# A two-stage layer on one core: the attention half's engine orders from a table of steps with due times

## The reference

```
q_top, q_idx = top_k(x @ w_qr[g], 512);  queries    = x[q_idx]     # 512 of 1024 tokens
kv_top,kv_idx= top_k(x @ w_kvr[g],256);  key_values = x[kv_idx]    # 256 tokens
q = queries @ w_q[g].T;  k, v = split(key_values @ w_kv[g].T);  v *= sigmoid(kv_top)
k, v get one learned null row;  attn = softmax(q k^T / 8)          # 8 heads of 64
o = (attn v) @ w_out[g].T * sigmoid(q_top)
result[q_idx] += o / number of groups that chose the token; tokens chosen by none get null_token
```

## Time and profile before

| | us |
|---|---|
| median of 3 runs | 3996.88 (3987.88 to 4007.33) |
| profiled execution | 3995.63 |
| its span | 3994.3 |

### The profile page before, as it was taken

The page is one execution under the profiler, slowest core; times in us unless marked ns, Lnnn a source line. Parts: engine busy times, 40 slices in busy tenths (PEclk is TensorE's granted clock), DMA queues, the critical chain, the costliest instruction groups (busy, mean ns, idle before and its releaser), DMA issues. The chain is left out here.

```text
span 3994.3 us, 72425 instructions
## 1 busy us (share of the span) xinstructions
PE 3649.7 (91%) x28354; PEld 2154.7 (54%) x28354; DVE 2955.1 (74%) x5374; ACT 2549.6 (64%) x4781; POOL 1770.5 (44%) x1483
## 2 busy tenths in 40 slices
PE   4899999999999999998568899988999989999998
PEld 2455555555555555555335455555555555656554
DVE  4788888888888888879756666666766666767663
ACT  4677676777777776765335655657665666656565
POOL 0232323333232333323336777656555565555555
PEclk8899999999999999999779999999999999999998
DMA  4223332324233332332343433334333343333332
GB/s 122 69 72 82 76 74 51 85 72 86 72 86 69 78 78 59 77 70 47 62 74 64 96 66 74 73 69 101 67 74 72 80 90 77 70 65 76 70 64 36
DMA packets 297670, 294.28 MB, mean 74 GB/s; under 512 B 38664, under 2 KB 223624, under 8 KB 295281
## 3 DMA queue, kind: packets, MB, share of 16 engines
q1 hardware_dynamic: 241008, 186.70, 18.8%
q0 software_dynamic: 56320, 102.94, 14.7%
HBM read 176.19 MB, written 101.71 MB: 70 GB/s over the span
## 5 line engine op out<-in xcount | busy, mean ns | idle before, releaser
L1542 DVE SCALAR_TENSOR_TENSOR cv<-raw,taps,cv 128x512 f32<-128x512 f32 x480 | 427.2, 900 | 70.1 <-ACT cv L1950 66.7
L1792 DVE TENSOR_REDUCE smx<-pair 128x2 f32<-128x514 f32 x512 | 346.3, 683 | 87.5 <-PE pair L1330 70.8
L2231 POOL TENSOR_TENSOR ph<-pf,ph 128x512 f16<-128x512 f32 x256 | 307.5, 1202 | 211.2 <-ACT ph L2090 210.2
L1149 PE MATMUL pair<-xhT,whi 128*128 128x512 f16 x1280 | 383.1, 381 | 0.2
L1397 PE MATMUL pair<-whi,oT 128*128 128x512 f16 x1024 | 333.2, 388 | 1.1 <-issue 0.7
L2236 POOL TENSOR_TENSOR ohl<-of,ohl 128x256 f16<-128x256 f32 x256 | 184.6, 721 | 332.3 <-ACT ohl L2095 332.1
L1195 PE MATMUL pair<-whi,xhT 128*128 128x512 f16 x1024 | 325.7, 379 | 0.2 <-DVE gmask L1581 0.2
L1232 PE MATMUL pair<-ohi,yT 128*128 128x512 f16 x1024 | 318.8, 383 | 1.1 <-ACT yT L2007 1.1
L1289 PE MATMUL pair<-xq,whi 128*128 128x512 f16 x1024 | 313.5, 388 | 3.0 <-ACT kb L2022 3.0
L1731 DVE TENSOR_SCALAR_CACHE_REDUCE rjunk<-rbc,cst 128x640 f16<-128x640 f16 (+1 forms) x192 | 185.5, 966 | 175.8 <-DMA rbc<-rank 169.7
L1980 ACT ACTIVATE de<-de,cum 128x128 f32<-128x128 f32 x1024 | 309.7, 389 | 1.0
(11 more groups left out here) (248 smaller groups left out, 10441.1 us busy)
## 6 DMA issues: line engine op xcount, KB each, us to landing
de<-cum SPq DMA_DIRECT2D x64, 1024.0 KB, 9.3
rows<-rowt SPq DMA_DIRECT2D x16, 1040.0 KB, 5.4
xin<-x SPq DMA_DIRECT2D x16, 1024.0 KB, 7.4
y<-xin SPq DMA_DIRECT2D x16, 1024.0 KB, 4.5
y<-ob POOLq DMA_DIRECT2D x64, 256.0 KB, 4.3
rbc<-rank SPq DMA_DIRECT2D x64, 256.0 KB, 3.8
qb<-qa SPq DMA_DIRECT2D x32, 512.0 KB
ka<-ka SPq DMA_DIRECT2D x32, 256.0 KB
```

The costliest lines, as they stand in the source:

```text
L1149: ins = pe.matmul(bk[:], w[:, k, ws], xt[:, ha, k, :], start=n == 0, stop=n == 3 * KD - 1)
L1542: ve.scalar_tensor_tensor(c_[:], r_[:, t:t + BLK], taps[:, ct, t:t + 1], c_[:], ALU.mult, ALU.add).then_inc(done, 1)
L1792: ve.tensor_reduce(smx[:, qt, 2 * h2:2 * h2 + 2], sc[:, :, 0:NK + 1], AX.X, ALU.max)
L2231: po.tensor_tensor(p_[:, 1, 1], f[:, 1], p_[:, 0, 1], ALU.subtract).then_inc(S.plp, 1)
```

## The change

The attention half is recorded as PE steps alone (`Feed` into a `Record`), and the new `arrange_items` gives `Order` all other steps of all 32 items in one table, with durations, inputs, readers of banks and landing times. Every step of one name runs in the order of the table. `Order` gets `keep`: a reader of a bank is also due `KEEP` = 4.0 us after the end of the PE step that it reads; for the Mamba half it is 1e9. `route`, `split_weights`, `null_rows` and the `last_q`, `last_k`, `last_max` steps go. The VectorE copy of null key columns has its own name, `keys_null`; VectorE's half of the low probabilities is `low_v`; ScalarE's cast is a step `high_p` of its own. The share at which the maxima begin goes from -1.25 to -0.8 (end 1.1 as before), and in the prologue the rows of item 1 come behind the maxima of item 0.

```diff
--- before.py
+++ after.py
 SCALE = DH ** -0.5
 LAG = 2
 SLOP = 0.7
+KEEP = 4.0
...
-    def __init__(self, plan, done, taken=(), between=()):
+    def __init__(self, plan, done, taken=(), between=(), keep=1e9):
+        self.keep = keep
...
-        follow = {}
-        for step, (_, _, after, _, _) in self.nodes.items():
+        follow, held = {}, {}
+        for step, (_, us, after, seats, _) in self.nodes.items():
             for a in after:
                 follow.setdefault(a, []).append(step)
+            for _, readers in seats:
+                for r in readers:
+                    held[r] = starts[step] + us + self.keep
 
         def last_start(step):
             if step not in starts:
                 end = min((last_start(f) for f in follow.get(step, ())), default=t + 100.0)
+                end = min(end, held.get(step, end))
                 starts[step] = end - self.HOP - self.nodes[step][1] - self.nodes[step][4]
...
+def arrange_items(plan, line):
+    done = [("weight_low", 0, NSP - 1), ("nulls", 0), ("slot", 0)]
+    for j in range(RT):
+        done += [(name, 0, j) for name in ("rank", "gather", "row", "row_out")]
+    order = Order(plan, done, keep=KEEP)
+    latest = {}
+    def add(engine, us, step, after=(), seats=(), extra=0.0):
+        after = [a for a in after if a[1] >= 0]
+        if engine != "PE" and step[0] in latest:
+            after.append(latest[step[0]])
+        latest[step[0]] = step
+        order.add(engine, us, step, after, seats, extra)
+    def each(name, n, count):
+        return [(name, n, k) for k in range(count)]
+    def back_by(name, n, h, k):
+        return (name, *divmod(H * n + h - k, H))
+    seats = {"q": "q_low", "k": "k_low", "v": "v_low", "row": "row_out", "max": "max_out", "shift_turn": "shift_out",
+             "null_turn": "null_out", "score": "soft", "value": "norm_o", "oturn": "oturn_out", "out": "res"}
+    takes = {"q": 2.6, "k": 2.62, "v": 2.6, "row": 0.45, "max": 0.23, "shift_turn": 0.24, "null_turn": 0.24,
+             "score": 0.88, "value": 0.95, "oturn": 0.45, "out": 2.6}
+    for step in line:
+        name, n, k = (*step, 0)[:3]
+        if name == "row":
+            after = [("gather", n, k)]
+        elif name in "qkv":
+            after = each("row_out", n, RT) + [("weight_low", n // NB, NSP - 1)]
+        elif name == "max":
+            after = each("q_low", n, KD) + [("keys", n)] + ([("keys_null", n)] if n % NB < 2 else [])
+        elif name == "shift_turn":
+            after = [("shift", n)]
+        elif name == "null_turn":
+            after = [("null_split", n)]
+        elif name == "score":
+            after = each("k_low", n, KT) + [("q_again", n), ("shift_in", n)]
+        elif name == "value":
+            after = [("low_p", n, k), ("low_v", n, k), ("null_out", n), ("nulls", n // NB)] + each("v_low", n, KT)
+        elif name == "oturn":
+            after = [("o_low", n, H - 1)]
+        else:
+            after = [("oturn_out", n, k)]
+        add("PE", takes[name], step, after, [("pair" if name in ("max", "score") else "single", [(seats[name], *step[1:])])])
+    for g in range(1, G):
+        for k in range(NSP):
+            add("SP", 0.5, ("weight_in", g, k), [("weight_low", g, k - 2) if k > 1 else ("weight_low", g - 1, NSP - 1)], extra=4.0)
+            add("ACT", 1.25, ("weight_high", g, k), [("weight_in", g, k), ("out", NB * (g - 1) - 1, QT - 1)])
+            add("POOL", 1.3, ("weight_low", g, k), [("weight_high", g, k)])
+        add("SP", 1.0, ("null_in", g), [("nulls", g - 2)], extra=3.0)
+        add("DVE", 3.3, ("nulls", g), [("null_in", g), ("value", NB * (g - 1) - 1, H - 1)])
+    for b in range(NB):
+        for c in range(TPS):
+            add("POOL", 1.6, ("null_add", b, c), [("score", b, c)], extra=3.0)
+    for n in range(ITEMS):
+        if n:
+            for j in range(RT):
+                if j in (0, QT):
+                    add("SP", 0.5, ("rank_load", n, j // QT), [("rank", n, j - 1) if j else ("slot", n - 1)], extra=3.5)
+                add("DVE", 1.05, ("rank", n, j), [("rank_load", n, j // QT), ("rank", n, j - 1) if j else ("slot", n - 1)])
+            add("DVE", 0.2, ("slot", n), [("rank", n, RT - 1)] + each("store", n - NSLOT, QT) + each("qscore", n - 2, QT) + each("gather", n - 4, RT))
+            for j in range(RT):
+                add("POOL", 1.05, ("gather", n, j), [("slot", n), ("row", n - 1, j), ("row_out", n - 1, j)], extra=4.0)
+                add("ACT", 0.6, ("row_out", n, j), [("row", n, j), ("q", n - 1, KD - 1) if j < QT else ("v_low", n - 1, KT - 1)])
+        two = ("score", n - 2, H - 1)
+        for e in range(KD):
+            add("ACT", 1.2, ("q_out", n, e), [("q", n, e), two])
+            add("DVE", 1.4, ("q_low", n, e), [("q_out", n, e)])
+        add("SP", 0.5, ("q_again", n), each("q_out", n, KD) + [two], extra=4.5)
+        for e in range(KT):
+            add("ACT", 1.2, ("k_out", n, e), [("k", n, e), two])
+            add("DVE", 1.4, ("k_low", n, e), [("k_out", n, e)])
+            add("ACT", 0.7, ("v_out", n, e), [("v", n, e), ("row_out", n, RT - 1), ("value", n - 2, H - 1)])
+            add("DVE", 0.75, ("v_low", n, e), [("v_out", n, e)])
+        add("SP", 0.5, ("keys", n), each("k_out", n, KT) + [two], extra=4.0)
+        if n % NB < 2:
+            add("DVE", 1.2, ("keys_null", n), [("nulls", n // NB), ("max", n - 2, QT * H // 2 - 1)])
+        for k in range(QT * H // 2):
+            add("DVE", 0.84, ("max_out", n, k), [("max", n, k)] + [("null_p", n - 1)])
+        add("DVE", 0.5, ("shift", n), each("max_out", n, QT * H // 2) + [("shift_turn", n - 1), ("null_split", n - 1)])
+        add("DVE", 0.42, ("shift_out", n), [("shift_turn", n), ("shift_in", n - 1)])
+        add("SP", 0.5, ("shift_in", n), [("shift_out", n), two], extra=3.0)
+        add("ACT", 0.25, ("null_p", n), [("shift", n)])
+        add("DVE", 0.65, ("null_split", n), [("null_p", n), ("null_turn", n - 1)])
+        add("DVE", 0.42, ("null_out", n), [("null_turn", n), ("value", n - 2, H - 1)])
+        for h in range(H):
+            add("ACT", 1.05, ("soft", n, h), [("score", n, h), back_by("low_p", n, h, 2), back_by("low_v", n, h, 2)])
+            add("ACT", 1.05, ("high_p", n, h), [("soft", n, h), back_by("value", n, h, LAG + 1)])
+            add("POOL", 1.2, ("low_p", n, h), [("high_p", n, h)])
+            add("DVE", 1.0, ("low_v", n, h), [("high_p", n, h)])
+            add("DVE", 0.66, ("norm_o", n, h), [("value", n, h), back_by("o_low", n, h, 2)])
+            add("ACT", 0.42, ("o_high", n, h), [("norm_o", n, h)] + each("oturn", n - 1, QT))
+            add("POOL", 0.7, ("o_low", n, h), [("o_high", n, h)])
+        for qt in range(QT):
+            add("POOL", 1.05, ("qscore", n, qt), [("slot", n)] + each("res", n - 2, QT), extra=4.0)
+            add("ACT", 0.6, ("oturn_out", n, qt), [("oturn", n, qt), ("out", n - 1, qt)])
+            before = ("store", n, qt - 2) if qt > 1 else ("store", n - 1, QT - 2 + qt)
+            add("ACT", 0.7, ("res", n, qt), [("out", n, qt), before] + each("qscore", n, QT))
+            add("POOL", 1.6, ("store", n, qt), [("res", n, qt)] + each("store", n - NB, QT) + (each("null_add", n, TPS) if n < NB else []), extra=4.0)
+    order.run()
...
-    def split_weights(g):
-        for k in range(NSP + 2):
-            if k > 1:
-                yield ("weight_high", g, k - 2)
-                yield Pause(0.3)
-                yield ("weight_low", g, k - 2)
-                yield Pause(0.5)
...
-        yield ("last_q", n)
...
-            if 0 < h <= QT:
-                yield ("qscore", n, h - 1)
...
     plan.append(("attention",))
-    plan.apart = False
-    for gen in (route(1), prepare(0), turn_rows(1), maxima(0)):
-        feed(gen, 1).to(1)
-        plan.settle()
+    plan.settle()
+    record = Record()
+    for gen in (prepare(0), maxima(0), turn_rows(1)):
+        Feed(gen, 1, record).to(1)
     for n in range(ITEMS):
         others = []
         if n:
-            others.append(Part(feed(turn_out(n - 1), QT * 0.43), -2.9, 6.0))
+            others.append(Part(Feed(turn_out(n - 1), QT * 0.43, record), -2.9, 6.0))
         if n + 1 < ITEMS:
-            others.append(Part(feed(prepare(n + 1), 20.8), 0, 1.8))
-            others.append(Part(feed(maxima(n + 1), 10.2), -1.25, 1.1))
+            others.append(Part(Feed(prepare(n + 1), 20.8, record), 0, 1.8))
+            others.append(Part(Feed(maxima(n + 1), 10.2, record), -0.8, 1.1))
         if n:
-            others.append(Part(feed(finish(n - 1), 10.4), -1.0, 1.0))
+            others.append(Part(Feed(finish(n - 1), 10.4, record), -1.0, 1.0))
         if n + 2 < ITEMS:
-            others.append(Part(feed(route(n + 2), 2 * RT + 3), 0, 1.8))
-            others.append(Part(feed(turn_rows(n + 2), RT * 0.43), -1.9, 1.25))
-        if n < NB:
-            others.append(feed(null_rows(n), TPS))
-        if n % NB == 2 and n // NB + 1 < G:
```

(23 more changed lines are left out.)

## The result

The changed kernel takes 3891.9 us against 3993.2 us: ratio 0.974, 95% interval 0.971 to 0.977. The forecast was 3919, within 3868 to 3972. The profiled execution took 3891.2 us, 104.4 less than that of before.

A forecast was written before the change was run, and what follows sets the result against it. TensorE is busy 91%; the attention half loses 97.3 us against quiet items. Savings of 39 + 15 + 12 + 12 = 78 us off the profiled 3995.6 give 3917.6, plus 1.3 for the median: 3919 us, range 3868 to 3972.

The forecast's parts named there:

- Weights: Items splitting the next group's weights: of 56.9 us lost, 39 us go as pieces spread over ScalarE's idle time.
- Items with null rows: Five items where GpSimd adds null rows lose 17.7 us; two thirds, 12 us, were to go.
- Quiet items: Rank compares waiting for loads in VectorE's queue: 0.4 us less per item, 12 us over 31.
- Null keys and the rest: Maxima's waits for VectorE's null-key copy, 14 us, plus 1 us for the first two items: 15 us saved.
- Maxima earlier: Maxima's share from -1.25 to -0.8: taken as 0, with a key-copy margin of 0.2 us.
- the early maxima's rival: Key copy starts 1 us later, so the first maximum waits 1 us in each of 31 items: 3950 us, 12%.
- Banks: Banks given on when their reader ends in the table, not after a fixed hold: 0, bounds -5 and +31 us.
- Start and end: Item 1's rows move behind item 0's maxima: 0, within 3 us either way; the drain stays.
- no interval above 62 us: Sign for the weights gain: no interval between TensorE's shift transposes, which mark the items, exceeds 62 us.
- this sign of being wrong: ScalarE's weight scaling still waiting over 2 us each for its DMA would show the forecast wrong.
- GpSimd's busy sum: Sign in the changed kernel's profile: GpSimd's and ScalarE's busy sums stay as before.
- The rival from the Trainium skill: VectorE's low-probability halves blocked behind GpSimd's on shared ports, 0.4 us per head: 4020 us, slower, 7%.

The follow-up runs named there:

- e1: Changed kernel with the maxima's share back at -1.25 instead of -0.8: 3937.4 us, ratio 0.995 to the kernel before.
- e4: Kernel before, with only the split of the next group's weights spread over four items instead of one: 3960.1 us, ratio 1.000.
- e9: Changed kernel with the next group's weight loads held back, so the split falls into item 2 as before: 3875.4 us, ratio 0.979.
- e3: Kernel before, with only the null-key copy made its own step ahead of the query projections: 3949.1 us, ratio 0.997.
- e6: Kernel before, with only the maxima's share changed from -1.25 to -0.8: 4005.5 us, ratio 1.012.
- e5: Changed kernel as it is, rerun on the follow-up chip: 3876.2 us, ratio 0.979 to the kernel before.
- e8: Changed kernel without the table's 0.15 us between same-engine steps of one name, and with the maxima's share at -1.25: 3867.1 us, ratio 0.976.
- e7: Changed kernel without the table's 0.15 us between steps of one name on the same engine: 3854.9 us, ratio 0.974.
- e2: Changed kernel, but a free engine takes the attention step that was ready first, not the one due first: 3880.7 us, ratio 0.979.
- e11: Changed kernel with KEEP at 1e9, so bank readers are due only when the next step needs their result: 3873.0 us, ratio 0.978.
- e12: Changed kernel without the 0.15 us between steps of one name, and with GpSimd's table times as traced: 3866.7 us, ratio 0.966, on another chip.

## Why the prediction was right, and where it wasn't

The sign and size are right; the gain was 104 us in the profile where 78 were forecast. The size is in part luck. The forecast put the share of the maxima at nothing, and with the old share the same table gains 22 us (e1), not 78: the new share hid a loss in the table that the forecast didn't know of. By its terms:
- **Weights, 39 us.** Measured 50 in the split items: 81.5 + 73.4 + 72.7 = 227.6 against 57.5 + 60.8 + 59.7 = 178.0. Most pieces now lie in items before these: group 1's in front of the first mark (nine) and in item 0 (seven), those of the other groups in item 9 or 17 (eleven) and 10 or 18 (four). Items 9 and 17 are 2 to 3 us over a quiet one. Against quiet items of 56.0, about 15 us stay of 57, so the net is 42. The reason given, spreading over idle time, was wrong as such: in the changed kernel eleven of 16 pieces stand in one item, spread by hand they gain nothing (e4), held back they lose nothing (e9). What the prediction said of SyncE's line, that whatever is queued behind the weight loads waits too, is what e4 shows. (A third of the 57 us is 19, not the 18 in the sum.)
- **Items with null rows, 12 us.** 302.2 to 288.8 for five items is 13.4, of which 4.5 is the quiet items' own gain: 8.9.
- **Quiet items, 12 us.** 56.9 to 56.0 is 0.9 each; 28 if every item gained as much. This term was too small by half. I had looked for it in the rank loads. They do stop VectorE less: 7 waits, 12.6 us, in place of 56 and 144.5 over most of the same stretch. But the idle time of TensorE in these items hardly fell, 2.0 to 1.9 us; the busy time did, 54.9 to 54.1, at a granted clock of 1.00 both times. Counted from start to start of the matmuls, as time beyond the spacing that they have without a stop, an item stood still for 3.4 us before and 2.5 after. The waits of the row transposes (0.55), of the output transposes (0.5) and most of those of the value steps (0.4) went, the score's wait for the shift fell by 0.3, and 0.85 came for the maxima. The chain of the shift, which I said would stay, lost 11 us in all (29.5 to 18.1).
- **Null keys and the rest, 15 us.** By difference 99.6 - 42 - 9 - 28 = 21, so this figure has the errors of the other three in it. The null-key copy is in no wait of the changed kernel. Alone it gives 10 (e3).
- **Maxima earlier, 0. This step failed.** The key copy, on which I spent the working, costs 6.9 us in six waits, and the early maxima's rival with it did not come. But the share is not neutral: +46 us alone, -61 us in the new order, -12 in the new order without the 0.15 us. I counted the packets (in a quiet item they came as 2, 3, 2, 2, 2, 3, 2) and the waits of the order before, and didn't ask where the new table would put VectorE's other steps between the maxima.
- **Banks, 0.** Two things that cancel in part: 29.5 us of waits for query banks gone (14.0 of them in the three split items, and counted there), 25 us of waits for maxima banks come.
- **Start and end, 0.** +2.7 (within the 3 us said) and -7.5.

Of what would show it: no interval above 62 us (the longest is 60.8), VectorE's wait for rank loads under 40 us, TensorE's idle 83.5 instead of 145.2 us (62 less; 60 to 80 was said). ScalarE's scaling waits for its DMA once in the intervals, 2.3 us, and four times just before them, 9.8 us, at the first weights of group 1; so this sign of being wrong did show, but only there. GpSimd's busy sum did not stay: 1159.6 against 1106.5 us in the intervals.

The parts don't add. Against 3960: table with the old share -22 us (e1), share in the old order +46 (e6), both -84 (e5). Without the 0.15 us: table with the old share -93 (e8), both -105 (e7). What the share is worth hangs on the order of the other engines, and the other way round.

The rival from the Trainium skill (SBUF — State Buffer, "SBUF: two separate sides") did not come to pass, but its collision is there, on the other engine. The changed kernel's halves of the low probabilities, GpSimd's and VectorE's, over the attention:

```profile
L2305 POOL TENSOR_TENSOR ph<-pf,ph x247: 1146/1460/2022, 2085.8 to 3826.0; 128x512 f16<-128x512 f32 x124
```

```profile
L1896 DVE TENSOR_TENSOR ph<-pf,ph x247: 677/693/2836, 2086.1 to 3827.2; 128x512 f16<-128x512 f32 x124
```

VectorE's median is the 0.69 us of a free one, and 84 of 247 take over 1 us, as before (87). GpSimd's median is 1.46 us. Before, it lay at 1.16:

```profile
L2231 POOL TENSOR_TENSOR ph<-pf,ph x247: 1143/1157/1744, 2074.1 to 3923.3; 128x512 f16<-128x512 f32 x124
```

Both halves wait for one cast and mostly start together now: a head's two halves overlap in 183 of 247 cases (108 before). Where VectorE's starts first, 123 times, it takes 0.69 us and GpSimd's 1.66 (medians). Where GpSimd's starts first, 60 times, GpSimd's takes 1.20 and VectorE's 1.14. Before, GpSimd's started first in 99 of the 108, and VectorE's took 1.44. The Trainium skill (same page and section) says that whoever starts first keeps the shared ports for the whole instruction and the other blocks; the longer durations of the second agree with it, but the traces show the duration, not the lock. Summed over the heads, GpSimd's halves take 54 us more than before, which is as much as its busy time in the intervals grew (53), and VectorE's 3 us less.

## What to carry to other kernels

In a list scheduler, look at what a free engine may take in the instant between two steps of a chain: 0.15 us of assumed delay let a 1.1 us step in before an urgent one, and taking it away gave 21 us. A schedule from readiness and durations made the weight split and the null keys cheap without anyone spreading them by hand; due times and bank due times on top gave nothing here (e2, e11). Look at the engine that issues the DMAs as at the others: a large load that waits for its buffer there held a small urgent one back for 6 us (e4). And a share or delay tuned under one order must be tried again under the next: the same number was worth +46, -61 and -12 us.

## What was not expected of the hardware

The kernel before took 3993 us (median) on the first chip, 3959 to 3960 on the two of e1 to e11 and 4005 on that of e12, 1.1% apart, while its runs on one chip lie within some 0.5%. The changed kernel differs by 0.4% between the first chip and that of e5. What differs between the chips is not shown.
